# Four PSUM banks for a group's scores, issued ahead of the values; bank 5 holds values and a transposition in turn; q and its transposition share bank 6

## The reference, cut to what matters

```python
def ln(x, g): ...                                   # LayerNorm over the last axis
xn = ln(x, g_norm)                                  # x: (8, 256, 128)
q = (xn @ Wq).reshape(b, n, 16, 64)                 # 16 heads of 64
k, v = split(xn @ Wkv)                              # one k and v for all heads; plus one null key and value
q = l2norm(q) * q_scale;  k = l2norm(k) * k_scale
sim = einsum(q, k) * 8 + attn_bias                  # bias: relative positions through a small MLP
attn = softmax(where(causal | ~mask, -max, sim))
y = ln((attn @ v).reshape(b, n, 1024) @ Wout, g_out)
out = x + quantised_ffn(y)                          # gate, up, down of width 352; int8 scales over all of y and h
```

## Time and profile before

| | |
|---|---|
| median of 3 runs | 310.94 us (310.54 to 310.96) |
| the profiled execution's own time | 309.61 us |
| its span in the profile | 307.8 us |
| busy: PE, PEld, DVE, ACT, POOL | 85%, 68%, 79%, 73%, 67% |
| mean granted TensorE clock | 0.975 |

### The profile page before, as it was taken

The page is one execution under the profiler, slowest core; times in us unless marked ns, Lnnn a source line. Parts: engine busy times, 40 slices in busy tenths (PEclk is TensorE's granted clock), DMA queues, the critical chain, the costliest instruction groups (busy, mean ns, idle before and its releaser), DMA issues.

```text
span 307.8 us, 7322 instructions
## 1 busy us (share of the span) xinstructions
PE 262.3 (85%) x2176; PEld 207.9 (68%) x2176; DVE 242.8 (79%) x976; ACT 224.9 (73%) x771; POOL 206.6 (67%) x393
## 2 busy tenths in 40 slices
PE   0767699999899989999998999899999998876251
PEld 0326578888688868877886888688878877561040
DVE  2978658788878888887888788868787876659985
ACT  1265678897889788978897888878888887437661
POOL 2786677679777877788789778887888755211401
PEclk9999699999999999999999999999999999999958
DMA  6369000000000000000000000000000020000005
GB/s 144 64 163 254 3 1 2 1 2 1 2 1 2 1 4 2 0 2 2 2 0 3 2 2 0 2 1 3 2 1 3 1 72 1 2 0 0 0 2 142
DMA packets 13084, 6.89 MB, mean 22 GB/s; under 512 B 1954, under 2 KB 12914, under 8 KB 13043
## 3 DMA queue, kind: packets, MB, share of 16 engines
q1 hardware_dynamic: 12466, 6.13, 8.0%
q10 hardware_dynamic: 576, 0.26, 0.4%
HBM read 5.31 MB, written 1.07 MB: 21 GB/s over the span
## 4 chain that ended last, share of the span: by engine, by line
PE 50%; DVE 21%; POOL 14%; issue 7%; ACT 5%; DMA 1%; ACTq 0%; POOLq 0%; DVEq 0%
PE bank L777 13%; PE bank L809 10%; PE bank L794 9%; PE bank L747 6%; POOL prob L415 5%; DVE score L1119 4%; PE bank L642 4%; POOL rq L370 3%; PE bank L658 3%; ACT prob L522 2%; DVE hmax L1252 2%; DVE kz L968 2%; DVE oT L1289 2%; DMA g0b<-in_L_cond_g_dram 1%; POOL rstd L370 1%
## 5 line engine op out<-in xcount | busy, mean ns | idle before, releaser
L522 ACT ACTIVATE prob<-score,negmax 128x258 f32<-128x258 f32 (+1 forms) x256 | 114.8, 454 | 30.3 <-DVE negmax L1119 30.1
L415 POOL TENSOR_SCALAR prob<-prob,rrow 128x258 f32<-128x258 f32 x254 | 109.2, 447 | 40.7 <-DVE rrow L1127 37.5
L1119 DVE CUSTOM_DVE_ANT_0 score<-bank,bias 128x258 f32<-128x258 f32 (+1 forms) x256 | 76.6, 355 | 20.9 <-PE bank L777 20.8
L532 ACT COPY pT<-bank 128x384 f32<-128x384 f32 x128 | 58.1, 480 | 15.3 <-PE bank L809 15.3
L777 PE MATMUL bank<-kT,qT 64*128 64x258 f32 (+1 forms) x512 | 60.1, 354 | 4.4 <-DVE negmax L1119 4.0
L777 PEld LDWEIGHTS bank<-kT,qT 64*128 64x128 f32 x512 | 44.6, 188 | 20.1 <-DVE negmax L1119 11.8
L809 PE MATMUL bank<-ident,prob 128*128 128x128 f32 x384 | 55.3, 280 | 1.0 <-ACT pT L532 1.0
L370 POOL TENSOR_TENSOR rq<-qn,neghalf 128x8 f32<-128x8 f32 x32 | 54.1, 1691 | 2.7
L809 PEld LDWEIGHTS bank<-ident,prob 128*128 128x128 f32 x384 | 43.7, 143 | 10.0 <-issue 1.7
L794 PE MATMUL bank<-pT,val 128*64 128x256 f32 (+1 forms) x512 | 48.7, 332 | 1.0 <-ACT pT L532 0.8
L522 ACT ACTIVATION_READ_ACCUMULATOR prob<-score,negmax 128x1 f32 x256 | 49.4, 193 | 0.0
(11 more groups left out here) (161 smaller groups left out, 340.2 us busy)
## 6 DMA issues: line engine op xcount, KB each, us to landing
bias<-relative_table SPq DMA_DIRECT2D x8, 256.0 KB, 5.3
out_dram<-prob SPq DMA_DIRECT2D x4, 256.0 KB, 3.0
X<-in_x_dram SPq DMA_DIRECT2D x1, 896.0 KB, 12.1
prob<-in_L_cond_Wq_dram SPq DMA_DIRECT2D x1, 512.0 KB, 5.5
wout<-in_L_cond_Wout_dram SPq DMA_DIRECT2D x1, 512.0 KB, 13.3
prob<-in_L_ffn_w_down_dram SPq DMA_DIRECT2D x1, 176.0 KB, 2.4
X<-in_x_dram SPq DMA_DIRECT2D x1, 128.0 KB, 4.1
prob<-in_L_ffn_w_gate_dram SPq DMA_DIRECT2D x1, 128.0 KB, 2.0
```

Of the source, the lines that this page charges most:

```text
L415: pool.tensor_scalar(prob[:, par, h, cols], prob[:, par, h, cols], rrow[:, par, h, t:t + 1], 1.0, ALU.mult, ALU.mult).then_inc(normed, 1)
L522: act.activation(prob[:, par, h, cols], score[:, h % 4, cols], ACT.Exp, scale=-1.0, bias=negmax[:, par, h, t:t + 1], accum_out=rowsum[:, p ...
L532: act.copy(pT[:, h % 4, :], trans_ps[h % 2][:, 0:3 * P]).then_inc(pT_ready, 1)
L1119: dve.tensor_tensor_reduce(score[:, h % 4, c0:c0 + w], ps[:, c0:c0 + w], bias[:, h, 0:w], -1.0, -3.0 * NEG, ALU.add, ALU.min, negmax[:, pa ...
```

## The change

Where the banks go after: 0 to 3 take the scores of the four heads, so both pairs are issued back to back at the group's start. Banks 4 and 5 (one tensor, `trans`) take the transpositions; the values go into **bank 5** as well (`val_ps`), so `turn` of head 1 waits for `oT_copy` of the values that were issued just ahead. The last 128 columns of banks 4 and 5 (`tails`) take the once-a-batch products, made inside `turn`. Bank 6 holds q and its transposition in turn, so `q_make` waits for `qT_evac`. On ACT, `q_square` and the exponentials of heads 2 and 3 of the group before stand at the group's start. On DVE, `q_norm2` and `invert` of heads 2 and 3 of the group before stand there, and `oT_copy` follows head 1's scores. The subtraction for `wql` goes from DVE to POOL, and the scaled copy of yT from DVE to ACT. `y_products` is split around `qT_make`. The last group's four transpositions have banks 0 to 3.

```diff
-        score_ps, trans_ps = bank[0:2], bank[2:4]
-        val_ps, q_ps, qT_ps, misc = bank[4], bank[5], bank[6], bank[7]
+        score_ps, trans_ps = bank[0:4], bank[4:6]
+        val_ps, q_ps, misc = bank[5], bank[6], bank[7]
+        tails = trans[:, :, 3 * P:4 * P]
...
 (POOL, group)
+                if s.kT is not None:
+                    k_power(s.kT)
+                if s.g == 2 and s.prev is not None:
+                    y_power(s.prev)
                 if s.quarter is not None and s.quarter >= 4:
                     q_power(s.quarter, s.quarter % 4)
...
+                if s.turned is not None:
+                    normalise(heads(s.turned)[2:4] if s.live else heads(s.turned)[2:3])
...
 (ACT, group)
+                if s.quarter is not None and s.quarter >= 4:
+                    q_square(s.quarter, q_ps)
+                if s.turned is not None:
+                    exponent(heads(s.turned)[2])
+                    exponent(heads(s.turned)[3])
                 if s.live:
                     exponent(heads(s.at)[0])
...
+                if s.live:
                     exponent(heads(s.at)[1])
+                if s.turned is not None:
+                    pT_evac(s.turned, 2)
+                    pT_evac(s.turned, 3)
...
 (PE, scores and turn)
-                if g > 0:
-                    pe.wait_ge(scored, 2 * g)
+                banks = score_ps[2 * pair:2 * pair + 2]
+                if g >= GH:
+                    pe.wait_ge(scored, 2 * (g - 2))
...
+                if i == 1 and s.summed is not None:
+                    pe.wait_ge(oT_ready, s.summed + 1)
+                if i < 2:
+                    low_make(s, i)
+                if i == 2:
+                    low_out(s)
...
 (PE, group)
+                if s.summed is not None:
+                    y_products(s.summed, 1)
+                if s.g == 1 and s.prev is not None:
+                    y_null(s.prev)
+                if s.turned is not None:
+                    turn(s, 2)
+                    turn(s, 3)
...
                 if s.made is not None:
+                    pe.wait_ge(qT_ready, s.made)
...
 (DVE, group)
+                if s.kT is not None:
+                    k_normalise(s.kT)
+                if s.turned is not None:
+                    invert(heads(s.turned)[2:4])
...
+                if s.g == 2 and s.prev is not None:
+                    y_normalise(s.prev)
                 if s.live:
...
                     score_pair(heads(s.at)[0:2])
+                if s.summed is not None:
+                    oT_copy(s.summed)
```

More of the change, by code:

```diff
@@ L499, in _ @@
             mlp_turned(0)
-            kv_evac(0, misc)
+            kv_evac(0, halves(misc))
             mlp_silu(1)
@@ L571, in group @@
+                if s.null is not None:
+                    null_evac(s.null)
+                if s.g == 1 and s.next is not None:
+                    v_copy(s.next)
                 if s.first and s.g == 1:
@@ L674, in _ @@
             pe.wait_ge(consts, 3)
-            xT_make(0, misc)
+            for t in range(2):
+                xT_make(0, t, halves(misc))
             mlp_turn(0)
@@ L681, in _ @@
             pe.wait_ge(wkv_ready, 1)
-            kv_make(0, misc)
+            for t in range(2):
+                kv_make(0, t, halves(misc))
             pe.wait_ge(wq_ready, 1)
@@ L691, in _ @@
             pe.wait_ge(kv_ready, 1)
-            kT_make(0, misc)
+            pe.wait_ge(kz_ready, 1)
+            pe.transpose(misc[:, 2 * P:3 * P], kz[:, 2, :], ident[:, :])
+            for t in range(2):
+                kT_make(0, t, halves(misc))
             q_make_first(2)
@@ L852, in group @@
                     q_make(s.made, s.made % 4, s.made // 4 % 2, q_ps)
[L853 to L859 removed]
+                if s.first and s.g == 1:
+                    null_output()
                 if s.at == GB * B + 1:
@@ L888, in ffn @@
             def ffn():
-                yT_make(B - 1)
+                for t in range(2):
+                    yT_make(B - 1, t)
                 keep_busy(8, q_ps)
@@ L1192, in group @@
-                if s.at >= 2:
-                    oT_copy(s.at - 2)
-                if s.live:
-                    score_pair(heads(s.at)[2:4])
-                    invert(heads(s.at)[0:2])
+                if s.summed is not None:
+                    oT_copy(s.summed)
+                if s.quarter is not None and s.quarter >= 4:
+                    q_normalise(s.quarter, s.quarter % 4, q_ps)
+                if s.live:
+                    score_pair(heads(s.at)[2:3])
+                if s.quarter is not None:
+                    qT_evac(s.quarter, s.quarter % 4, s.quarter // 4 % 2)
@@ new lines, in group @@
+                if s.live:
+                    score_pair(heads(s.at)[3:4])
+                    invert(heads(s.at)[0:2])
+                if s.at == 0:
+                    q_normalise(3, 3, q_ps0[3])
+                    x_stats(2)
+                if s.at == 1:
+                    null_values()
+                if s.at == 2:
+                    x_normalise(2)
+                if s.g == 0 and s.b > 1:
+                    yT_absmax(s.b - 2)
+                if s.g == 0 and s.prev is not None and s.b + 2 < B:
+                    x_normalise(s.b + 2)
```

363 lines of the change are left out of this document (172 added, 191 removed).

## The result

| | before | after |
|---|---|---|
| median | 310.93 us (310.54 to 310.96) | 336.08 us (334.71 to 336.92) |
| the profiled execution's own time | 309.61 us | 334.71 us |

The ratio is 1.081 (95% interval 1.076 to 1.086). The median stands 1.37 above the profiled execution (forecast: 1.3).

What follows compares the result with a forecast made beforehand. PE was taken to bound the kernel before, and a loop through PE, ACT and DVE the changed one. 309.6 - 3.5 + 20.4 + 2.5 = 329.0 us; the median, 1.3 above, gives 330 us, range 317 to 338.

Steps and rivals of the forecast that it cites:

- the side that had 0.87: The outcome that the changed kernel is slower, given chance 0.87.
- the loop as worked out: Round from q_make through ACT, DVE and PE to the next q_make: 7.68 us a group; 319 to 335 us, chance 0.78.
- a falling clock: Rival: PE's idling lowers the clock in one group of ten, doubling PE work there: +8, 339 us; chance 0.07.
- start: Before group 2: idle PE and low clock regained, against wql on POOL; -3.5 us taken.
- groups: 27 groups, from group 2's start to group 29's: 219.9 us against 199.5, +20.4 us.
- end: From group 29's start to the end of y_null: 31.7 us against 29.2, +2.5 us, between 0 and 4.
- The step that decided: PE's transposition of head 1 waits for oT_copy to free bank 5, 4.39 us after q_make's end.
- only the copy counts: Rival: exponentials finish before DVE needs them; PE waits 0.33 us a group for oT_copy; median 308 us, chance 0.10.
- Never waiting: Rival: PE never waits in the groups; 1.1 us less a batch, 298 us in all, chance 0.05.
- once-a-batch terms: Extra work or delay on the loop in g = 0, 1 and 2, together 12.5 us in 27 groups.
- The term that was put at nothing: q and qT sharing bank 6 costs nothing: qT_evac ends at about 6.5 us, q_make starts at 6.9.
- my walk: Steps followed through groups 29 to 31: 6.5 us a group, 0.73 more where y is normalised.

Runs made afterwards that it cites:

- experiments 3 and 4: Changed kernel plus an unread 256-column ACT copy in groups 4 to 31: between q_square and the exponentials, 343.53 us; between two copies of transposed probabilities, 336.34 us.
- experiment 1: Changed kernel with DVE's oT_copy moved between the scores of head 0 and head 1: 325.15 us.
- 9: Changed kernel with the values' matmuls between the two pairs of scores on PE: 335.93 us.
- experiment 8: Changed kernel with oT_copy after head 0's scores, head 2's exponential before q_square, y_normalise behind oT_copy, k_norm2 and k_power a group earlier, x_power behind normalise: 320.29 us.
- experiment 10: Kernel of experiment 8 with the values' matmuls between the two pairs of scores on PE: 320.28 us.
- 6: Changed kernel with oT_copy between the scores of heads 0 and 1, head 2's exponential ahead of q_square, and y_normalise behind oT_copy: 324.26 us.
- experiment 12: Changed kernel with q_square behind both exponentials on ACT and q_norm2 behind invert on DVE: 358.30 us in the profiled execution, 355.80 in another.
- experiment 7: Kernel before with only wql's subtraction moved from DVE to POOL: 308.13 us, ratio 0.993.
- experiment 11: Kernel before with wql's subtraction on POOL and k_normalise behind qT_evac on DVE in g = 2: 306.99 us, ratio 0.987.

## Why the prediction was right, and which terms were off

The forecast was 330 us, in a range of 317 to 338. The measured 336.08 lies in it, on the side that had 0.87. It lies 1.1 above the 319 to 335 of the loop as worked out, and is inside the range because that one had been stretched for a falling clock; the clock did fall, once, at a cost of 1.6 us (below). The three terms, start, groups and end, missed by -0.9, +3.4 and +3.2 us.

**The step that decided held.** "Only then may PE transpose head 1, because bank 5 still holds the values": the wait is there in all 30 groups from group 2 to group 31, 34.4 us in all. Its cause is the order on ACT and DVE, shown by experiments 3 and 4 (the same work on and beside the path: 7.45 against 0.3 us), by 1 (10.9 us won without taking work away), and by 9 (an earlier input to the copy wins nothing). The rival *only the copy counts* gave 0.33 us a group; this is close to the wait of 0.30 that experiment 8 shows once the order is mended. It is a true wait, but it ruled neither in the changed kernel nor, as experiment 10 shows, in experiment 8's. *Never waiting* appears in no version.

**The group: 7.85, not 7.68.** Measured in g = 3, from one end of `q_make` to the next: 0.03 to `q_square`, 0.50 until the exponentials, 1.89 with them and the start of `invert`, 0.16 to the scores, 1.12, the copy's 0.69 and 0.14 to PE, and 3.32 on PE. The largest miss is the hand-over from the copy to PE: I took 0.05 from the earlier trace rows, it is 0.14. The next is `invert` to the scores, 0.16 where rows 4 gave 0.10. Together they are 0.15 of the 0.17. The once-a-batch terms came out at 0.40 in g = 0, 0.81 in g = 1 and 0.61 in g = 2 (8.25, 8.66 and 8.46 less 7.85), 1.82 a batch where I had 1.97. A batch: 33.2 us, forecast 32.7. The 27 groups last from 38.34 to 261.68, 223.3 us: +23.8, forecast +20.4.

**The term that was put at nothing.** The prediction has it that sharing bank 6 costs nothing, since `qT_evac` ends at about 6.5 us of the group and `q_make` starts at 6.9. In the group shown it ends at 6.77 (152.37 + 0.69, less 146.29), and `q_make` starts at 6.90. So in the changed kernel it holds, but with 0.13 us to spare instead of 0.4. In the kernel before, `q_make` could follow `qT_make` at once; now the transposition and its copy stand in q's round. That this is what keeps experiment 8 above the kernel before is argued from the rows: no run gives q and its transposition a bank each under the new order.

**The start: -4.4, forecast -3.5.** Group 2 starts at 38.34 instead of 42.77. The clock stayed at 1.00. `wql` takes POOL 2.37 us, as estimated (2.5), but PE waits only 0.30 and 0.16 us for the `normalise` behind it.

**The end: +5.7, forecast +2.5.** From group 29's start to the end of `y_null` it is 34.9 us. Here the forecast had the right sign and half the size. PE and DVE near group 30, in the kernel after:

```profile
274.93 0.87 PE L890 MATMUL trans<-ident,prob 128*128 128x128 f32 x3 [2.25 <-ACT pT L559]
275.60 1.92 PE L794 MATMUL bank<-wout,oT 128*128 128x128 f32 x8
```

```profile
271.59 0.18 DVE L1189 RECIPROCAL rrow<-rowsum 128x4 f32<-128x4 f32 x1 [1.75 <-ACT prob L548]
272.33 0.73 DVE L1204 TENSOR_SCALAR yn<-bank,omv,ors 128x128 f32<-128x128 f32 x2 [0.57 <-POOL ors L388]
```

Two things were not in my walk. `y_normalise` waits 0.57 us for its own power, which comes behind `normalise` and two memory fills (0.31 and 0.12 us) on POOL. And after 2.25 us of idle the eight matmuls of `y_products` last 1.92 us instead of the normal 1.06. What that clock cost can be read against experiment 1, where PE idled 1.69 us in the same place and the clock stayed up: from the wait's end to group 31's scores 268.24 - 266.24 = 2.00 us there, 278.55 - 274.93 = 3.62 here. So 1.6 us of the 3.2 that were missing are the clock and 0.6 the power; the remaining 1.0 lies elsewhere: groups 29 and 31 last 7.49 and 7.69 us where the walk had 6.5 each, and what follows takes 10.3 us where it had 11.5. Why was not looked into. The clock's fall was a rival (+8) for the whole attention; it came once, at the end. That it came only once was luck and not worked out: the fall in one group of ten that the rival priced would have put the time outside the range.

**The sum.** -4.4 + 23.8 + 5.7 = +25.1, and the profiled executions differ by 334.71 - 309.61 = 25.1.

**What was said to show.** PE busy 26 to 27 of 30 us: 25.8. The wait of head 1's transposition some 0.8 us: 0.83 in g = 0 and 0.98 in g = 3, up to 1.52 in g = 2. `invert` waiting for ACT: 29.1 us in 28 waits. But the trace names the wanted releaser, `oT`, in none of the five rows of waits: POOL's normalising and ACT's copies end at about the same time. In g = 0 PE went on at 125.45, before POOL's next `normalise` had begun (125.63), and 0.15 after the copy's end.

**The rule on banks.** The Trainium skill (Perfetto Trace Analysis, Optimizing Tensor Performance, Matmuls) wants independent groups of matmuls to rotate through different banks. The runs agree on both sides: the scores with four banks wait for no bank in mid-attention, and with bank 5 shared PE waits 0.30 us for the copy at its best (experiment 8, g = 3). The prediction called the rule's second half the loop; the rule prices only the copy, and the rest of the loop came from the orders on ACT and DVE.

**Left open.** The values can't have a bank of their own in this layout, since all eight are in use; that was not tried. Experiment 8's batch lasts 31.28 us, and 29.96 in the kernel before. Of the difference of 1.32 us one half is idle time of PE (1.74 against 1.08 us, of which the waits named above are 1.53); the other half is busy time (29.54 against 28.88), which was not taken apart. Whether `q_square` ahead of the exponential would shorten q's round in experiment 8's order was not tried either.

## What to carry to other kernels

When an order is written out by hand, follow the round from an instruction back to itself through every engine's queue: the longest such round is the least that a stage can take, however idle each engine is. An instruction that waits, queued ahead of others that are ready, puts its own wait into all of them (`q_square` ahead of two ready exponentials). An edit that shortens a round is worth only the distance to the next longest one, so look for that one first (here q's, which took gain from experiments 1, 6 and 10); and a change made of many parts should be timed by its parts, since here a good one (`wql`, 2.4 us less than the runs beside it) was hidden by a bad one.

## What the runs showed of the hardware that was not expected

- PE started 0.14 to 0.15 us after a DVE copy had ended that freed its bank, in each of four groups looked at. The nearest row of before had 0.05; there the matmul waits for the copy's output, not for its bank.
- Sixteen score matmuls in a row take 1.52 us from start to start (146.22 to 147.74). In two parts of eight, with the values between them, they take 0.86 each; this is 0.20 more in all.
- The clock after a pause: 2.25 us idle in group 30 was followed by a lower clock, and 1.69 us in the same place (experiment 1) was not. In mid-attention, experiment 12 has 1.97 us of idle at 114.85 without a lower clock and 1.96 us at 150.07 with one. At the start, after 1.63 us of idle in the same place, experiment 7 shows a granted clock of 0.70 from 35 to 40 us and experiment 11 shows 1.00. Pauses of these lengths don't settle it by themselves.
- The releaser that a row of waits names can be a bystander: five rows of the kernel after name POOL or ACT for a wait that ended, in each of the four groups looked at, 0.14 to 0.15 us after DVE's copy.
